# Expert tile loops with 79 and 23 tiles instead of 80 and 24, the last seven of each written out

## The reference

```python
# layer 1 (L1f): 8 experts, each token goes to 1, hidden width 1024
for e in range(8):
    ye = relu(x @ w1[e] + b1[e]) @ w2[e] + b2[e]
    out = out + where(expert_idx == e, ye * expert_w, 0)
# layer 2 (L2f): 16 experts, each token goes to 4, hidden width 256
h, u = einsum(x, gate_w), einsum(x, up_w)
y = einsum(silu(h) * u, down_w)
routed = einsum("etd,te->td", y, combine)      # combine: 4 shares a token, the rest 0
out = routed + (silu(x @ sh_gate_w) * (x @ sh_up_w)) @ sh_down_w
```

## Time and profile before

| | us |
|---|---|
| median of three runs | 1816.34 |
| the three runs | 1816.02 to 1816.98 |
| the profiled execution, its own time | 1812.46 |
| its span in the profile | 1810.7 |
| PE busy in the span | 1375.2 |
| DVE busy | 977.8 |
| ACT busy | 684.9 |
| POOL busy | 363.1 |

### The profile page before, as it was taken

How to read it: one execution, slowest core, us unless ns; L and a number is a source line. 1 busy time by engine, 2 the same in 40 slices (tenths; PEclk the granted TensorE clock), 3 DMA queues, 4 the chain that set the end, 5 groups by cost and what they waited for, 6 DMA issues and landing times. The chain is left out here.

```text
span 1810.7 us, 32769 instructions
## 1 busy us (share of the span) xinstructions
PE 1375.2 (76%) x10700; PEld 1159.9 (64%) x10709; DVE 977.8 (54%) x2405; ACT 684.9 (38%) x1355; POOL 363.1 (20%) x452
## 2 busy tenths in 40 slices
PE   4999657768699965999999979899998951102464
PEld 3777535667599964888877868599997941101232
DVE  3777654646422225555555546422222735888785
ACT  2555442500344411333333323355553252402454
POOL 1000000012122210222222223266664300001000
PEclk9999867889599997999999979699998986555787
DMA  3000020751211116111111020122222414120001
GB/s 95 19 17 13 16 70 1 242 203 24 68 36 35 32 37 197 59 44 43 43 43 43 1 79 4 36 93 90 93 91 77 173 57 109 13 56 1 0 0 47
DMA packets 96893, 108.65 MB, mean 60 GB/s; under 512 B 27888, under 2 KB 83952, under 8 KB 96496
## 3 DMA queue, kind: packets, MB, share of 16 engines
q1 hardware_dynamic: 84240, 79.35, 14.5%
q0 software_dynamic: 9984, 27.28, 4.8%
q10 hardware_dynamic: 2592, 1.05, 0.2%
HBM read 85.55 MB, written 20.97 MB: 59 GB/s over the span
## 5 line engine op out<-in xcount | busy, mean ns | idle before, releaser
L3452 PEld LDWEIGHTS L2f_bank<-L2f_xT,L2f_w_tile 128*128 128x128 f32 x1280 | 157.6, 194 | 4.0
L3452 PE MATMUL L2f_bank<-L2f_xT,L2f_w_tile 128*128 128x128 f32 x1280 | 158.0, 277 | 0.0
L758 POOL TENSOR_TENSOR L2x_probs<-L2x_probs,L2x_inv_sum 128x512 f32<-128x512 f32 x64 | 65.3, 1041 | 288.2 <-DVE L2x_inv_sum L1025 288.2
L3528 DVE TENSOR_TENSOR L2f_hT<-L2f_gate_h,L2f_bank 128x256 f32<-128x256 f32 x80 | 33.7, 421 | 151.9 <-ACT L2f_gate_h L3498 151.9
L3485 ACT COPY L2f_w_tile<-L2f_w_up 128x1024 f32 x80 | 83.7, 1047 | 45.6 <-issue 35.2
L3452 PEld LDWEIGHTS L1f_bank<-L1f_xT,L1f_w_tile 128*128 128x128 f32 x768 | 90.8, 194 | 1.1
L3452 PE MATMUL L1f_bank<-L1f_xT,L1f_w_tile 128*128 128x128 f32 x768 | 90.9, 277 | 0.0
L3390 POOL DMA_INDIRECT L2f_y_rows<-L2f_xn,L2f_put_row x80 | 79.2, 990 | 55.9 <-DVE L2f_xn L3544 52.7
L3382 POOL DMA_INDIRECT L2f_rows<-L2f_x_rows,L2f_take_row x80 | 77.8, 972 | 49.3 <-SPq L135 23.9
L3469 PE MATMUL L1f_bank<-L1f_w_down,L1f_hT 128*128 x384 | 86.7, 379 | 0.0
L1007 DVE TENSOR_REDUCE L2x_top<-L2x_bank 128x4 f32<-128x512 f32 x64 | 43.9, 686 | 79.0 <-PE L2x_bank L827 79.0
(11 more groups left out here) (652 smaller groups left out, 3379.4 us busy)
## 6 DMA issues: line engine op xcount, KB each, us to landing
L1f_w_up<-in_L_ffn_w SPq DMA_DIRECT2D x16, 512.0 KB, 10.2
L1f_w_down<-in_L_ffn_w SPq DMA_DIRECT2D x16, 512.0 KB, 9.9
L2f_got<-L2f_y_rows SPq DMA_DIRECT2D x16, 512.0 KB, 4.1
L2f_w_up<-in_L_ffn_gate_w SPq DMA_DIRECT2D x16, 256.0 KB, 2.9
L2f_w_up<-in_L_ffn_up_w SPq DMA_DIRECT2D x16, 256.0 KB, 3.2
L2f_w_down<-in_L_ffn_down_w SPq DMA_DIRECT2D x16, 256.0 KB, 3.6
x<-in_x SPq DMA_DIRECT2D x4, 512.0 KB, 7.6
L0x_ctx<-in_ctx SPq DMA_DIRECT2D x16, 128.0 KB, 2.1
```

The lines of the kernel that those rows point to most:

```text
L758: nc.gpsimd.tensor_tensor(probs[c][:, :, :], probs[c][:, :, :], inv_sum[:, c, :][:, :, None].to_broadcast([P, 4, P]), ALU.mult).then_inc(s ...
L3452: x = nc.tensor.matmul(products(j, m), w_tile[j][:, at:at + P], xT[j][:, k * P:(k + 1) * P], start=(k == 0), stop=(k == KT - 1))
L3528: nc.vector.tensor_tensor(hT[j][:, 0:F], gate_h[j][:, 0:F], bank[2 + j][:, F:2 * F], ALU.mult).then_inc(q["h"], 1)
```

## The change

The rounding to a multiple of four goes. `over_tiles` leaves its loop earlier and writes out the rest, four tiles and what is over. For 79 tiles that is 4 written out, 17 iterations of four, 7 written out (before: 4, 18, 4). For 23 tiles it is 4, 3 iterations, 7 (before: 4, 4, 4). Every engine that uses it (PE, ACT, DVE) has it so. POOL's written-out list is one gather and one scatter shorter, and its last wait counts for each of the four buffers the tiles that used it.

```diff
@@ over_tiles
     with eng.Fori(0, (n - 8) // 4) as i:
         for u in range(4):
             body(u, i * 4 + (4 + u))
-    for t in range(n - 4, n):
+    for t in range(n - 4 - n % 4, n):
         body(t % 4, t)
@@ ExpertLoads.__init__
         self.tiles = (B * P * K + E * (P - 1)) // P
-        self.tiles += -self.tiles % 4
@@ routed_experts, POOL's stream of the tile block
             for j in range(4):
-                pool.wait_ge(q[f"stored{j}"], 16 * S // 4)
+                pool.wait_ge(q[f"stored{j}"], 16 * len(range(j, S, 4)))
```

## The result

The changed kernel took 1803.09 us in the median of six runs (1798.62 to 1807.47), the kernel before 1816.41 (six runs): a ratio of 0.9934, 95% interval 0.9919 to 0.9949, or 12.0 us less (9.3 to 14.7). Forecast were 1806.1 us and 10.2 us less, which lies inside that interval. The profiled execution took 1798.62 us, its span is 1796.9.

The account below looks back on a forecast made before the run. PE was taken to bound both tile blocks, busy almost throughout; -7.24 (L1f tile), -2.87 (L2f tile) and -0.1 (routing) sum to -10.2 us, so 1816.34 becomes 1806.1 us, range 1801.8 to 1810.2.

Parts of the forecast that it names:

- The main step: Tile blocks of L1f and L2f: one tile less saves one distance between expands on PE, 7.24 and 2.87 us.
- Moved bodies at 0: L1f and L2f: three tile bodies moved from the loop to the written-out end cost 0.
- The jump back: Loops of L1f and L2f: one jump less an engine a stage gives 0; it delays ACT by 0.08 us, unnoticed by PE.
- the scatter at the end: End of the tile blocks: the last scatter waits for the last result, so the 7.5 us tail keeps its length.
- the work of ACT, DVE and POOL at 0: L1f and L2f: these engines' work for a tile lies beside PE's, so its removal or move counts 0.
- The routing: Routing arrays 79 wide for 80, mainly in L2f: -0.1 us taken, bounds -0.3 and +4.2.
- The +4.2 us on the other side: L2f's routing: an odd count could cost DVE its fast handling of 16-bit data, 4.2 us at most.
- The sum of 10.2 us: Whole kernel: -7.24 for L1f's tile, -2.87 for L2f's and -0.1 for the routing.
- nothing is late next: the loads and sums behind the barrier just start earlier: Behind the tile blocks: following loads and sums only move forward, with nothing gained or lost there.
- Carrying the difference over to the forecast: Whole kernel: the median's 3.9 us above the profiled execution was taken as the same after the change.
- Badly lying loops: Rival: loops behind L1f at new addresses wait for instruction fetches, 1.7 us a jump, 25.5 us, 1831.6 us in all; chance 0.03.
- The clock in L3f: Rival: L3f's alternation between 1.2 and 2.4 GHz changes, up to 10.4 us either way; chance 0.08, half each way.

Follow-up runs that it names:

- e9: Kernel before, plus eleven unread matmuls a batch in PE's idle time in L3f; ratio 0.9950 to the kernel before.
- e11: The changed kernel measured a third time, on a third chip; ratio 0.9932 to the kernel before, 12.6 us less.
- e1: The change with only layer 1 dropping its tile (23 and 80 tiles); ratio 0.9946 to the kernel before, 9.8 us less.
- e2: The change with only layer 2 dropping its tile (24 and 79 tiles); ratio 0.9987 to the kernel before, 2.4 us less.
- e5: The change with one tile more taken away in each stage (22 and 78 tiles); ratio 0.9873 to the kernel before, 23.1 us less.
- e7: The kernel before, unchanged, run and profiled once more; ratio 0.9997 to the kernel before.
- e4: The changed kernel measured a second time; ratio 0.9928 to the kernel before, 13.1 us less.
- e3: Kernel before with its 24 and 80 tiles, loop one iteration shorter, last eight tiles written out; ratio 0.9998 to the kernel before.
- e6: The change's loops over 23 and 79 tiles, but routing and arrays kept 24 and 80 wide; ratio 0.9925 to the kernel before, 13.6 us less.
- e10: Layer 1's tile alone dropped (23 and 80 tiles), measured again on a third chip; ratio 0.9942 to the kernel before, 10.7 us less.
- e12: e1 plus two more gathers by POOL in L1f into buffers nothing reads; ratio 0.9953 to the kernel before, 8.5 us less.
- e8: The change plus eleven unread matmuls a batch in PE's idle time in L3f; 1793.04 us, ratio 0.9875 to the kernel before.

## Why the prediction was right, and where it was short

The main step held. Each tile was worth the distance of the expands on PE: the loops show 7.24 us in every profile and 2.87 in all but e9 to e11 (see the last section), one tile less gave it once (e1, e2), a second tile gave it again (e5). From the first expand to the last it is 164.83 us in L1f of e7 and 157.58 in e4, 7.25 less, and in L2f 227.98 and 224.93, 3.05 less. Reading the distance between tiles rather than a busy share was enough, because PE doesn't idle there.

Moved bodies at 0: right, shown by e3. The jump back, the scatter at the end, the work of ACT, DVE and POOL at 0: right as far as the distances on PE show; the runs resolve no less than 2 us.

The routing: I took -0.1 us, the lower bound of the terms being -0.3; it was -0.3 (18.4 us for 18.7 and 18.8). The matmuls fell by at least all that their columns would give, more than I allowed. The +4.2 us on the other side had nothing to it: 488 ns for 632 elements.

The sum of 10.2 us was short by 2 to 3 us in the runs: four sets of them, the result, e4, e11 and e6, have 12.0, 13.1, 12.6 and 13.6 us less. Three of the four intervals reach down to 10.2, but all four values lie above it. The profiles show about 1 us of that, or 2 if L3x is left out. Comparing the kernels with 24/80 tiles directly with those with 23/79, L1f is 7.6 us shorter, L2f 3.1 (without the chip of e9 to e11), L2x 1.7 (377.4 to 375.7) and L3x 1.5 longer, about 11 us together. L3x follows neither count (224.0 with 23/80 in e10, 221.6 with 24/79 in e2), so I take it for scatter.

The step that was mis-sized is "nothing is late next: the loads and sums behind the barrier just start earlier". In most profiles they also take less time. From the last result of L1f to the start of L2x it is 24.6 to 24.8 us with 24 tiles, and 23.9 to 24.3 with 23 or 22, but for e6 with 24.65. The first loaded rows of L1f's sum reach DVE 2.07 us after their issue instead of 2.67 (661.44 to 663.51, and 672.62 to 675.29); it is 1.9 to 2.1 in all with fewer tiles and 2.7 to 2.8 with 24, except in e3, which has 24 tiles, the last eight written out, and 2.10. So this half microsecond does not go with the tile count alone. The larger part is the head of L2x, where PE mostly starts on its first weights sooner than behind 24 tiles (6.5 to 7.4 us behind its first transposes, not 8.0 to 8.6). In the profiles with 24 tiles L2x took 378.2 to 378.4 us four times and 374.7 once; in nine with 23 or 22 it took 373.7 to 376.8. That it goes with layer 1's tile is borne out by its return in e10 to e12 and contradicted by one profile of the fourteen (374.7 us with 24 tiles); it isn't proven, and what would make it so is open. It isn't the width of the arrays (e6) or the count of indirect DMAs (e12), and e3, with other code positions, did not bring it about.

The one outlier, 374.7, is in the profiled execution of the kernel before. I wrote that no stage explains why it was 3.9 us under the median. Against the other profiles of its kind L2x is 3.6 us shorter, but L1x and L1f are 1.6 and 1.0 us shorter than in e7 too. L1x lies ahead of all that the change touches, and it is 119.4 to 119.9 us in three profiles (before, the change, e1) and 121.1 to 121.8 in all others, in e4 and e10 too, which are the kernels of the change and of e1. So that execution was quick in several stages, by a cause that I don't know. In the first pair of profiles L2x therefore gives only 1.0 of the 13.8 us. Carrying the difference over to the forecast was right for the median: after the change it is 4.5 us.

The rivals. Badly lying loops: excluded by e3 and by L2x's unchanged 22.0 us a batch. The clock in L3f: the pattern shifted by one pair in the first profile after, but so it did in e7, the kernel before, and L3f stayed within 129.6 to 132.1 us, so its alternation neither vanished nor filled all batches. But the mechanism is real: e8 took the 10 us that the prediction had put on it. The unforecast luck sat in L0f, 4.5 us.

## What to carry to other kernels

Where one engine has no idle time through a loop, an iteration less was worth the distance between iterations, and the last ones can be written out to get rid of a rounded count; this holds only as long as another engine doesn't take over. Between two profiles of almost the same kernel compare stages, untouched ones first: they show how much is luck before anything is explained. And where a stage's matmuls come in two lengths by turns, look at the granted clock: some idle work on PE can be worth more than the change under study.

## What the runs showed that I had not expected

The 10 us of L3f's alternating clock could be had for eleven matmuls a batch. e8 beats both kernels: 1793.04 us.

One of the four chips ran the same kernel before in 1849.5 us instead of 1816 (e9 to e11). All of it is in L2f, 424 to 428 us for 391 to 394; the other stages agree within their scatter. ACT in order of time in L2f in e11:

```profile
1214.04 0.38 ACT L3497 ACTIVATE L2f_gate_h<-L2f_bank 128x256 f32<-128x256 f32 x1
...
1214.60 1.04 ACT L3484 COPY L2f_w_tile<-L2f_w_up 128x1024 f32 x1
1221.54 0.38 ACT L3497 ACTIVATE L2f_gate_h<-L2f_bank 128x256 f32<-128x256 f32 x1 [5.89 <-DMA L1f_got<-L1f_y_rows]
1221.82 0.37 ACT L3490 COPY L2f_xT<-L2f_bank 128x256 f32<-128x256 f32 x1
```

ACT stands for 5.89 us, and its activations are 7.50 us apart where 2.87 is the rule. PE stops with it: its expands on either side are 6.58 us apart. Such stops come several times in the block; the DMA named had long been done, so the trace doesn't say what ACT waited for. The length of L2f is nearly the same in the three kernels profiled there (424.0 to 428.3 us), so the ratios can still be read, with a scatter of some microseconds in that stage.
